# Self-attention in a two-block transformer kernel: one accumulator copy on ScalarE, and both halves of the first probability tile on GpSimd

## The chip, the core and the metric

The kernel runs on one core of a Trainium2 chip, in one launch. The metric is the time of one execution on the device, in microseconds (us). The engines are named as the profile names them: PE is TensorE (PEld its weight loads), DVE is VectorE, ACT is ScalarE, POOL is GpSimd, SP is SyncE, which here only issues DMAs. Each engine works through its own instructions in program order; between engines only semaphores set the order.

## What is computed

Eight sequences of 512 positions with 256 channels go through a cross-attention block (16 heads of 16 channels, context of 64 positions, with an MLP), then through a second block with self-attention, cross-attention and a gated MLP. The change lies in the self-attention of the second block, which is

```python
def _attn(xq, xc, Wq, Wk, Wv, Wo, bo):      # HEADS = 16, D_HEAD = 64
    q = (xq @ Wq).reshape(B, N, HEADS, D_HEAD)
    k = (xc @ Wk).reshape(B, S, HEADS, D_HEAD)
    v = (xc @ Wv).reshape(B, S, HEADS, D_HEAD)
    scores = jnp.einsum('bnhd,bshd->bhns', q, k) * scale
    attn = jax.nn.softmax(scores, axis=-1)
    out = jnp.einsum('bhns,bshd->bnhd', attn, v).reshape(B, N, HEADS * D_HEAD)
    return out @ Wo + bo

x = _attn(_ln(x, g1, b1), _ln(x, g1, b1), Wq1, Wk1, Wv1, Wo1, bo1) + x
```

with B = 8, N = S = 512.

## The kernel before, in words

**Numbers as pairs.** Every matrix product is made from float32 operands that are split in two: a rounded upper half (type fp32r) and the rest, the operand minus its rounded half. A product is three matmuls, upper x upper, upper x rest, rest x upper (`mm3`, lines 146 to 148). So every operand needs a rounded copy and a subtraction. The rounding of a tile is done by ScalarE (`act_copy`, line 156) or GpSimd (`pool_copy`, line 159), the subtraction by VectorE (`dve_rest`, line 162) or GpSimd (`pool_rest`, line 165).

**Steps.** The self-attention is a loop of steps (`loop3`), each for one sequence and one pair of heads: 8 x 8 = 64 steps. Step s works on three pairs at once: for u = s + 1 it projects queries, keys and values and takes the maxima of the scores; for t = s it makes scores less maxima and exponentials, in four tiles j = 0 to 3 of 128 keys by 2 x 512 queries; for d = s - 1 it multiplies the probabilities with the values. Normalization and output projection follow one to two steps later. The output projection is done for two pairs together, in two halves: the first in an odd step behind the value products of j = 3, the second in the next even step at j = 1. So steps of even and odd number differ. Every eighth step also makes a layer norm for a later sequence, and another one its statistics.

**TensorE**, in a step: score products for j (lines 1348 and 1352; the second adds the negated maxima), q projection, value products j = 0, k projection, values' projection, value products j = 1, in even steps a half of the output projection, four times the full scores for the maxima (line 1386; the first in bank 2 after j = 1), the value products of j = 2 and 3, in odd steps the other half of the output projection, and last four transposes of the maxima (line 152). The first product of line 1386 waits for the keys' rests (`k3_lo`); the output product of an odd step waits for the normalized halves (`o3_lo`).

**ScalarE**: rounded queries and keys (four copies of 64x512 after the exponential of j = 0), exponentials (line 1500), rounded values, the rounded probabilities of j = 1 and 2, and at j = 3 copies of the two accumulators: PSUM bank 4 holds the outputs of the first head in rows 0 to 63 and the sum of its probabilities in row 64, bank 5 the second head's outputs in rows 64 to 127 and its sum in row 0. Two copies of one row each go first and release the DMA of the sums (`d3_sum`), two copies of 64 rows gather both heads into one tile `OA` (`d3_out`). Behind them come the two copies of the negated maxima, which wait for the transposes, and the next step's queries.

**VectorE**: rests of the queries (line 1569), the reciprocals of the sums (1615), the subtraction for probability tile 3 of the step before, rests of the keys (1573) and of the values, the subtraction for tile 0 of this step, in even steps the residual addition (1636), maxima of two score tiles (1588), the subtraction for tile 1, two more maxima, in odd steps the residual addition, the subtraction for tile 2.

**GpSimd**: two copies of the rounded keys (64x512), the rounded probabilities of tile 0, then the normalization of an earlier pair: a multiplication by the reciprocals when these have landed (line 1697), a rounded copy and a rest; last the rounded probabilities of tile 3. The reciprocals are spread over 64 rows each by a DMA to memory and back (lines 1303 and 1307).

An exponential of tile j waits for the subtraction of tile j - 2, because there are two buffers `pst3` for the unrounded exponentials. The functions that the change touches, with what calls them:

## Time and profile before

| | us |
|---|---|
| median of 3 runs (2293.42 to 2293.97) | 2293.42 |
| the profiled execution's own time | 2292.69 |
| its span, first to last instruction | 2290.9 |
| TensorE busy | 2121.8 (93%) |
| VectorE busy | 1608.8 (70%) |
| ScalarE busy | 1482.3 (65%) |
| GpSimd busy | 1070.5 (47%) |

Busy times are those of the whole kernel, of which the self-attention is about half. "Idle before" in a row is the time for which an engine did nothing ahead of an instruction, with the engine, tile and line that ended it. A busy time of a VectorE or GpSimd row includes what the instruction waited inside itself.

### The profile page before, as it was taken

To read this page: it belongs to the slowest core of one execution; us is meant where nothing else is said; L and a number is where in the kernel's file an instruction comes from. 1 tells how busy PE (TensorE), PEld (TensorE's weight loads), DVE (VectorE), ACT (ScalarE), POOL (GpSimd) and SP (SyncE) were. 2 spreads that over 40 slices of the span, in tenths; PEclk is the share of its full clock that TensorE was granted. 3 is DMA by queue.
4 is the path that set the end of the run, shared out by engine and by line. 5 is a ranking of instruction groups with operands and counts; after the bars stand their busy time and mean duration, and the time that the engine had idled before them with its cause. 6 is when DMAs were issued, how large, how long until landed. Compare 5 with 4: busy or idle time off the path is not lost. (4 is left out here: it accounts for less than half of the span.)

```text
span 2290.9 us, 31305 instructions
## 1 busy us (share of the span) xinstructions
PE 2121.8 (93%) x11628; PEld 1771.6 (77%) x11628; DVE 1608.8 (70%) x2345; ACT 1482.3 (65%) x2154; POOL 1070.5 (47%) x819
## 2 busy tenths in 40 slices
PE   6868999988899999999999999999997799999998
PEld 4657888876687778777777777777776689888987
DVE  5576767753787787777877778778776766666553
ACT  5546888754777777777777777777774355554431
POOL 2154544441354454454544545545454665656432
PEclk8989999998999999999999999999999999999999
DMA  6810000010000100001001000010004411111000
GB/s 212 297 43 5 22 22 22 20 66 33 19 24 16 37 15 24 24 15 34 15 15 34 15 29 24 15 33 15 24 26 165 138 44 53 56 56 47 10 10 19
DMA packets 84280, 102.67 MB, mean 45 GB/s; under 512 B 29664, under 2 KB 61152, under 8 KB 83616
## 3 DMA queue, kind: packets, MB, share of 16 engines
q1 hardware_dynamic: 84128, 100.66, 13.3%
q8 instruction: 93, 1.52, 0.3%
q14 instruction: 59, 0.48, 0.1%
HBM read 65.50 MB, written 33.82 MB: 43 GB/s over the span
## 5 line engine op out<-in xcount | busy, mean ns | idle before, releaser
L146 PE MATMUL PS<-R 128*128 128x512 f32 (+1 forms) x2944 | 1026.4, 349 | 77.1 <-DVE R L162 46.1
L148 PE MATMUL PS<-R 128*128 128x512 f32 (+1 forms) x2944 | 996.5, 338 | 0.0
L147 PE MATMUL PS<-R 128*128 128x512 f32 (+1 forms) x2944 | 995.8, 338 | 0.0
L146 PEld LDWEIGHTS PS<-R 128*128 128x128 f32 x2944 | 565.8, 192 | 189.9 <-DVE R L162 55.3
L156 ACT ACTIVATE R<-PS 64x512 fp32r<-64x512 f32 (+4 forms) x860 | 460.1, 548 | 239.7 <-PE PS L1805 129.4
L148 PEld LDWEIGHTS PS<-R 128*128 128x128 f32 x2944 | 565.1, 192 | 60.4
L147 PEld LDWEIGHTS PS<-R 128*128 128x128 f32 x2944 | 566.9, 193 | 54.4
L162 DVE TENSOR_TENSOR R<-F,R 128x1024 fp32r<-128x1024 f32 (+2 forms) x416 | 465.2, 1123 | 44.2 <-ACT R L156 22.4
L159 POOL TENSOR_SCALAR R<-F 128x1024 fp32r<-128x1024 f32 (+1 forms) x295 | 266.2, 904 | 284.0 <-DVE F L1958 149.3
L1500 ACT ACTIVATE F<-PS 128x1024 f32<-128x1024 f32 x256 | 263.1, 1028 | 170.3 <-DVE R L162 115.1
L159 POOL TENSOR_SCALAR R<-R 64x512 fp32r<-64x512 f32 x128 | 142.8, 1129 | 391.4 <-ACT R L156 391.4
L1588 DVE TENSOR_REDUCE F<-PS 128x2 f32<-128x1024 f32 x256 | 301.4, 1214 | 14.1 <-PE PS L1386 14.1
L162 DVE TENSOR_TENSOR R<-PS,R 128x512 fp32r<-128x512 f32 (+3 forms) x348 | 181.0, 542 | 160.9 <-ACT R L156 160.3
L165 POOL TENSOR_TENSOR R<-F,R 128x512 fp32r<-128x512 f32 (+2 forms) x126 | 229.6, 1824 | 31.0 <-ACT R L156 22.4
L1569 DVE TENSOR_TENSOR R<-PS,R 64x512 fp32r<-64x512 f32 x128 | 88.0, 688 | 220.1 <-ACT R L156 220.1
L156 ACT ACTIVATE R<-F 128x1024 fp32r<-128x1024 f32 (+2 forms) x246 | 200.5, 829 | 61.2 <-PE PS L148 56.0
L156 ACT ACTIVATE F<-PS 64x512 f32<-64x512 f32 (+3 forms) x280 | 160.2, 593 | 50.4 <-PE PS L148 40.5
L1386 PE MATMUL PS<-R 128*128 128x512 f32 x512 | 164.0, 402 | 7.2 <-ACT F L156 4.9
L1352 PE MATMUL PS<-R 128*128 128x512 f32 x512 | 162.7, 399 | 7.8 <-ACT R L156 6.5
L1348 PE MATMUL PS<-R 128*128 128x512 f32 x512 | 165.9, 405 | 2.6 <-ACT F L1500 2.6
L1134 POOL TENSOR_TENSOR F<-F 128x1024 f32<-128x1024 f32 x32 | 67.9, 2123 | 165.4 <-DVE F L1048 165.4
L1697 POOL TENSOR_TENSOR F<-F 128x512 f32<-128x512 f32 x64 | 82.7, 1292 | 119.6 <-DMA F<-sd 119.6
(89 smaller groups left out, 1990.9 us busy)
## 6 DMA issues: line engine op xcount, KB each, us to landing
F<-sd SPq DMA_DIRECT2D x128, 128.0 KB, 2.8
xs<-F SPq DMA_DIRECT2D x16, 512.0 KB, 2.6
F<-xs SPq DMA_DIRECT2D x16, 512.0 KB, 3.6
gd<-F SPq DMA_DIRECT2D x8, 768.0 KB, 3.6
vd<-F SPq DMA_DIRECT2D x8, 768.0 KB, 5.9
R<-gd SPq DMA_DIRECT2D x6, 1024.0 KB, 5.5
R<-vd SPq DMA_DIRECT2D x6, 1024.0 KB, 5.7
F<-in_x SPq DMA_DIRECT2D x8, 512.0 KB, 5.7
```

The costliest lines, as they stand in the source:

```text
L146: nc.tensor.matmul(o, L[0], Rr[0], start=start, stop=False, skip_group_check=share)
L147: nc.tensor.matmul(o, L[0], Rr[1], start=False, stop=False, skip_group_check=share)
L148: return nc.tensor.matmul(o, L[1], Rr[0], start=False, stop=stop, skip_group_check=share)
L156: return nc.scalar.activation(o, i, ACT.Identity, **k)
L159: return nc.gpsimd.tensor_scalar(o, i, 1.0, 1.0, ALU.mult, ALU.mult)
L162: return nc.vector.tensor_tensor(o, i, f32(hi), ALU.subtract)
L165: return nc.gpsimd.tensor_tensor(o, i, f32(hi), ALU.subtract)
L1348: nc.tensor.matmul(bank(h), ka[i][h][:, kk], qa[i][h], start=True, stop=False)
L1352: m = nc.tensor.matmul(bank(h), kb[i][h][:, kk], qb[i][h], start=False, stop=True)
L1386: m = nc.tensor.matmul(bank(b0 + h), qa[i][h][:, 128 * q:128 * q + 128], ka[i][h], start=True, stop=True)
L1500: nc.scalar.activation(pst3[n % 2], bank(0, 2), ACT.Exp, scale=0.125).then_inc(e3.sem, 1)
L1588: nc.vector.tensor_reduce(M3[:, q, 0:128:64], bank(b0, 2).rearrange("p (a b) -> p a b", a=2), AX.X, ALU.max).then_inc(b3_max.sem, 1)
```

## The change

It does three things. ScalarE copies both accumulators whole in one instruction, `OAB <- bank(4, 2)`, 128x1024, instead of four; `OA` is then bank 4 and `OB` bank 5, and the DMAs take the sums from row 64 of `OA` and row 0 of `OB` once this copy is done. GpSimd multiplies the two heads apart, rows 0 to 63 of `OA`, and rows 64 to 127 from `OB` into `OA`. And GpSimd makes tile 0 of the probabilities whole, the rounded copy and now the subtraction too, both ahead of the keys' copies; VectorE's subtractions for tiles 1 to 3 stay. The event `p_lo` becomes two, one for each engine. TensorE's and SyncE's instructions keep their order.

```diff
--- before.py
+++ after.py
@@ -411,6 +411,7 @@
             o3_s = [ra.pair(NT) for _ in range(2)]
             wk = fa.take(6 * 512)
             pst3 = [wk[:, 1024 * i:1024 * i + 1024] for i in range(2)]
+            OAB = wk[:, 2048:3072]
             OA, OB = wk[:, 2048:2560], wk[:, 2560:3072]
             RS3 = fa.take(NT)
             M3 = fa.take(4, 128)
@@ -1197,8 +1198,9 @@
         nm3_mm, nm3_neg = event("nm_mm", N3), event("nm_neg", N3)
         c3_mm, e3 = event("c_mm", 4 * N3), event("exp", 4 * N3)
 
-        p3_act, p3_pool, p3_lo = event("p_act", 2 * N3), event("p_pool", 2 * N3), event("p_lo", 4 * N3)
-        d3_mm, d3_sum, d3_out = event("d_mm", 4 * N3), event("d_sum", N3), event("d_out", N3)
+        p3_act, p3_pool = event("p_act", 2 * N3), event("p_pool", 2 * N3)
+        p3_lo_pool, p3_lo_dve = event("p_lo_pool", N3), event("p_lo_dve", 3 * N3)
+        d3_mm, d3_out = event("d_mm", 4 * N3), event("d_out", N3)
         rec3, mul3, o3_hi, o3_lo = event("rec", N3), event("o_mul", N3), event("o_hi", N3), event("o_lo", N3)
         o3_mm, o3_add = event("o_mm", N3), event("x_add", N3)
         sum3 = [event(f"sum_in{i}", N3, 16) for i in range(2)]
@@ -1255,6 +1257,12 @@
             pool.wait_ge(vw_hi, 2 * b - 4 + half)
             v = vw_b[b % 2][:, 4 * half:4 * half + 4]
             pool_rest(v[:, :, 1], f32(v)[:, :, 1], v[:, :, 0]).then_inc(vw_lo.sem, 1)
+
+        def wait_rest3(queue, n):
+            if n % 4 == 0:
+                queue.wait_ge(p3_lo_pool, n // 4)
+            else:
+                queue.wait_ge(p3_lo_dve, 3 * (n // 4) + n % 4 - 1)
 
         def tail3(s, j):
 
@@ -1307,9 +1315,9 @@
                             nc.sync.dma_start(RS3[64 * h:64 * h + 64, :], sd[k][512 * h:512 * h + 512]
                                               .partition_broadcast(64)).then_inc(in3[k].sem, 16)
                     if ok(d, N3) and j == 3:
-                        sp.wait_ge(d3_sum, d)
+                        sp.wait_ge(d3_out, d)
                         sp.wait_ge(rec3, d - 2)
-                        nc.sync.dma_start(SQ3[d % 2][0:64, :], OB[64:65, :]).then_inc(sum3[d % 2].sem, 16)
+                        nc.sync.dma_start(SQ3[d % 2][0:64, :], OA[64:65, :]).then_inc(sum3[d % 2].sem, 16)
                         nc.sync.dma_start(SQ3[d % 2][64:128, :], OB[0:1, :]).then_inc(sum3[d % 2].sem, 16)
                     e = s - 3
                     if j == 1 and ok(e, N3) and e % 8 == 7:
@@ -1387,7 +1395,7 @@
                 m.then_inc(b3_mm.sem, 1)
 
             def values(d, j):
-                pe.wait_ge(p3_lo, 4 * d + j)
+                wait_rest3(pe, 4 * d + j)
                 pe.wait_ge(v3_lo, 2 * (d // 2) + j // 2)
                 if j == 0:
                     pe.wait_ge(d3_out, d - 1)
@@ -1496,7 +1504,7 @@
             def exponent(t, j):
                 n = 4 * t + j
                 act.wait_ge(c3_mm, n)
-                act.wait_ge(p3_lo, n - 2)
+                wait_rest3(act, n - 2)
                 nc.scalar.activation(pst3[n % 2], bank(0, 2), ACT.Exp, scale=0.125).then_inc(e3.sem, 1)
 
             def value(u):
@@ -1536,11 +1544,8 @@
                         act.wait_ge(d3_mm, 4 * d + 3)
                         act.wait_ge(sum3[(d - 1) % 2], 2 * ((d - 1) // 2) + 1)
                         wait_weights(act, "o1")
-                        act_copy(OB[64:65, :], bank(4)[64:65, :])
-                        act_copy(OB[0:1, :], bank(5)[0:1, :]).then_inc(d3_sum.sem, 1)
                         act.wait_ge(o3_lo, d - 1)
-                        act_copy(OA[0:64, :], bank(4)[0:64, :])
-                        act_copy(OA[64:128, :], bank(5)[64:128, :]).then_inc(d3_out.sem, 1)
+                        act_copy(OAB, bank(4, 2)).then_inc(d3_out.sem, 1)
                     if ok(u, N3) and j == 3:
                         act.wait_ge(nm3_mm, u)
                         act.wait_ge(c3_mm, 4 * (u - 2) + 3)
@@ -1574,12 +1579,12 @@
                                                 ).then_inc(k3_lo.sem, 1)
 
             def rests(n):
-                if 0 <= n < 4 * N3:
-                    if n % 4 in (1, 2):
+                if 0 <= n < 4 * N3 and n % 4 > 0:
+                    if n % 4 < 3:
                         dve.wait_ge(p3_act, 2 * (n // 4) + n % 4 - 1)
                     else:
-                        dve.wait_ge(p3_pool, 2 * (n // 4) + n % 4 // 3)
-                    dve_rest(P3[1][:, n % 4, :], pst3[n % 2], P3[0][:, n % 4, :]).then_inc(p3_lo.sem, 1)
+                        dve.wait_ge(p3_pool, 2 * (n // 4) + 1)
+                    dve_rest(P3[1][:, n % 4, :], pst3[n % 2], P3[0][:, n % 4, :]).then_inc(p3_lo_dve.sem, 1)
 
             def largest(u, q, b0):
                 dve.wait_ge(b3_mm, 4 * u + q)
@@ -1686,6 +1691,12 @@
                     for b_ in (6, 7):
                         pool.wait_ge(x_out[x_at(0, b_)], store_no[0, b_])
                 for j in range(4):
+                    if ok(t, N3) and j == 0:
+                        pool.wait_ge(e3, 4 * t)
+                        pool.wait_ge(d3_mm, 4 * (t - 1))
+                        pool_copy(P3[0][:, 0, :], pst3[0]).then_inc(p3_pool.sem, 1)
+                        pool.wait_ge(p3_pool, 2 * t)
+                        pool_rest(P3[1][:, 0, :], pst3[0], P3[0][:, 0, :]).then_inc(p3_lo_pool.sem, 1)
                     if ok(u, N3) and j == 0:
                         for h in range(2):
                             pool.wait_ge(k3_hi, 2 * u + h)
@@ -1694,16 +1705,23 @@
                         f = d - 1
                         pool.wait_ge(in3[f % 2], 2 * (f // 2) + 1)
                         pool.wait_ge(d3_out, f)
-                        nc.gpsimd.tensor_tensor(OA, OA, RS3, ALU.mult).then_inc(mul3.sem, 1)
+                        nc.gpsimd.tensor_tensor(OA[top, :], OA[top, :], RS3[top, :], ALU.mult)
+                        pool.wait_ge(o3_lo, f - 1)
+                        pool.wait_ge(p3_lo_pool, t) if more else pool.wait_ge(p3_pool, 2 * N3 - 1)
+                        if more and p == 5:
+                            pool.wait_ge(ln_rstd, 18 + b)
+                        if f == N3 - 1:
+                            pool.wait_ge(ln_nl, norm4[2][2])
+                        nc.gpsimd.tensor_tensor(OA[low, :], OB[low, :], RS3[low, :], ALU.mult).then_inc(mul3.sem, 1)
                         pool.wait_ge(mul3, f)
                         pool.wait_ge(o3_mm, 2 * ((f - 2) // 2) + 1)
                         pool_copy(o3_s[f % 2][0], OA).then_inc(o3_hi.sem, 1)
                         pool.wait_ge(o3_hi, f)
                         pool_rest(o3_s[f % 2][1], OA, o3_s[f % 2][0]).then_inc(o3_lo.sem, 1)
-                    if ok(t, N3) and j in (0, 3):
-                        pool.wait_ge(e3, 4 * t + j)
-                        pool.wait_ge(d3_mm, 4 * (t - 1) + j)
-                        pool_copy(P3[0][:, j, :], pst3[j % 2]).then_inc(p3_pool.sem, 1)
+                    if ok(t, N3) and j == 3:
+                        pool.wait_ge(e3, 4 * t + 3)
+                        pool.wait_ge(d3_mm, 4 * (t - 1) + 3)
+                        pool_copy(P3[0][:, 3, :], pst3[1]).then_inc(p3_pool.sem, 1)
                     for job in weights3_at(s, j):
                         pool_weight(job)
                     for _ in range(early4_pool.get(tail3(s, j), 0)):
@@ -1768,7 +1786,8 @@
             for i in loop4:
                 b = i // 4
                 if i == 2:
-                    sp.wait_ge(p3_lo, 4 * N3 - 1)
+                    wait_rest3(sp, 4 * N3 - 4)
+                    wait_rest3(sp, 4 * N3 - 1)
                     for k in range(4):
                         sp_weight(g5, k)
                     sp_load(3, 2, xs)
```

GpSimd in a step, before, from the keys' copies on (L159 R<-R) to the rounded copy of tile 3:

```order
L159 TENSOR_SCALAR R<-R 64x512 x2
L159 TENSOR_SCALAR R<-F 128x1024
L1697 TENSOR_TENSOR F<-F 128x512
L159 TENSOR_SCALAR R<-F 128x512
L165 TENSOR_TENSOR R<-F,R 128x512
L159 TENSOR_SCALAR R<-F 128x1024
```

GpSimd after; the first row holds the copy of tile 3 of one step and that of tile 0 of the next:

```order
L159 TENSOR_SCALAR R<-F 128x1024 x2
L165 TENSOR_TENSOR R<-F,R 128x1024
L159 TENSOR_SCALAR R<-R 64x512 x2
L1708 TENSOR_TENSOR F<-F 64x512
L1715 TENSOR_TENSOR F<-F 64x512
L159 TENSOR_SCALAR R<-F 128x512
L165 TENSOR_TENSOR R<-F,R 128x512
```

The copy of tile 0 moved from behind the keys' copies (L159 64x512 x2) to ahead of them, with a subtraction of 128x1024 (L165) behind it, and the multiplication (L1697) became two of 64x512 (L1708 and L1715).

VectorE in an even step before, from the rests of the queries (L1569) to the subtraction for tile 2:

```order
L1569 TENSOR_TENSOR R<-PS,R 64x512 x2
L1615 RECIPROCAL F<-F 128x8
L162 TENSOR_TENSOR R<-F,R 128x1024
L1573 TENSOR_TENSOR R<-PS,R 64x512 x2
L162 TENSOR_TENSOR R<-PS,R 128x4x64 x2
L162 TENSOR_TENSOR R<-F,R 128x1024
L1636 TENSOR_TENSOR F<-PS,F 128x512
L1588 TENSOR_REDUCE F<-PS 128x2 x2
L162 TENSOR_TENSOR R<-F,R 128x1024
L1588 TENSOR_REDUCE F<-PS 128x2 x2
L162 TENSOR_TENSOR R<-F,R 128x1024
```

VectorE in an even step after (its lines are numbered 5 higher, L1574 for L1569):

```order
L1574 TENSOR_TENSOR R<-PS,R 64x512 x2
L1620 RECIPROCAL F<-F 128x8
L162 TENSOR_TENSOR R<-F,R 128x1024
L1578 TENSOR_TENSOR R<-PS,R 64x512 x2
L162 TENSOR_TENSOR R<-PS,R 128x4x64 x2
L1641 TENSOR_TENSOR F<-PS,F 128x512
L1593 TENSOR_REDUCE F<-PS 128x2 x2
L162 TENSOR_TENSOR R<-F,R 128x1024
L1593 TENSOR_REDUCE F<-PS 128x2 x2
L162 TENSOR_TENSOR R<-F,R 128x1024
```

The L162 of 128x1024 between the values' rests (128x4x64) and the residual addition (L1641, before L1636) is gone; the one for tile 3 of the step before still stands behind the reciprocal and ahead of the keys' rests (L1578, before L1573).

## Rows read from the trace of the kernel before

**Rows 1.** Busy time in a stretch: us, each engine's busy us (x instructions), TensorE's clock, DMA.

```profile
573.40:1741.80 1168.40, 1119.05 (x5568) 901.96 (x5569) 905.03 (x1114) 880.11 (x1285) 564.65 (x472) 1.00 0.08 23
```

**Rows 2.** Waits, 800 to 1740 us: engine line waited for, us in total, times, longest us.

```profile
PEld PS L152 <- DVE F L1588: 29.0, 26, 1.7
...
PE PS L146 <- POOL R L165: 5.2, 9, 1.4
```

**Rows 3.** Timeline, VectorE, even step: start us, us, engine line op out<-in, [idle before].

```profile
1202.83 1.17 DVE L162 TENSOR_TENSOR R<-F,R 128x1024 fp32r<-128x1024 f32 x1
...
1206.38 1.21 DVE L162 TENSOR_TENSOR R<-F,R 128x1024 fp32r<-128x1024 f32 x1
1207.51 0.68 DVE L1636 TENSOR_TENSOR F<-PS,F 128x512 f32<-128x512 f32 x1
1208.11 2.35 DVE L1588 TENSOR_REDUCE F<-PS 128x2 f32<-128x1024 f32 x2
1210.37 1.82 DVE L162 TENSOR_TENSOR R<-F,R 128x1024 fp32r<-128x1024 f32 x1
```

**Rows 4.** Timeline, GpSimd, the same even step.

```profile
1202.78 2.29 POOL L159 TENSOR_SCALAR R<-R 64x512 fp32r<-64x512 f32 x2 [7.12 <-ACT R L156]
1205.03 1.05 POOL L159 TENSOR_SCALAR R<-F 128x1024 fp32r<-128x1024 f32 x1
1207.74 1.29 POOL L1697 TENSOR_TENSOR F<-F 128x512 f32<-128x512 f32 x1 [1.66 <-DMA F<-sd]
1209.12 0.62 POOL L159 TENSOR_SCALAR R<-F 128x512 fp32r<-128x512 f32 x1
1209.82 1.29 POOL L165 TENSOR_TENSOR R<-F,R 128x512 fp32r<-128x512 f32 x1
```

**Rows 5.** Timeline, ScalarE, the same even step.

```profile
1199.82 1.03 ACT L1500 ACTIVATE F<-PS 128x1024 f32<-128x1024 f32 x1
...
1213.63 2.27 ACT L156 ACTIVATE F<-PS 1x512 f32<-1x512 f32 x4
1215.92 2.41 ACT L156 ACTIVATE R<-PS 1x512 fp32r<-1x512 f32 x4
1218.36 1.03 ACT L1500 ACTIVATE F<-PS 128x1024 f32<-128x1024 f32 x1
```

**Rows 6.** Timeline, TensorE, the same even step.

```profile
1206.77 0.63 PE L1386 MATMUL PS<-R 128*128 128x512 f32 x2
...
1214.52 0.65 PE L152 MATMUL PS<-F 128*128 128x128 f32 x4 [0.93 <-DVE F L1588]
```

**Rows 7.** Timeline, VectorE, the odd step behind it.

```profile
1221.36 1.17 DVE L162 TENSOR_TENSOR R<-F,R 128x1024 fp32r<-128x1024 f32 x1
1222.56 1.41 DVE L1573 TENSOR_TENSOR R<-PS,R 64x512 fp32r<-64x512 f32 x2
...
1228.30 1.43 DVE L162 TENSOR_TENSOR R<-F,R 128x1024 fp32r<-128x1024 f32 x1
```

**Rows 8.** Timeline, GpSimd, the same odd step.

```profile
1226.67 1.29 POOL L1697 TENSOR_TENSOR F<-F 128x512 f32<-128x512 f32 x1 [2.05 <-DMA F<-sd]
...
1228.75 2.13 POOL L165 TENSOR_TENSOR R<-F,R 128x512 fp32r<-128x512 f32 x1
```

**Rows 9.** Timeline, TensorE, the same odd step.

```profile
1224.25 0.62 PE L1386 MATMUL PS<-R 128*128 128x512 f32 x2
...
1230.41 0.39 PE L148 MATMUL PS<-R 128*128 128x512 f32 x1
1231.03 0.36 PE L146 MATMUL PS<-R 128*128 128x256 f32 x1 [0.23 <-POOL R L165]
```

**Rows 10.** Timeline, all engines, a step with a layer norm.

```profile
1287.49 2.37 POOL L165 TENSOR_TENSOR R<-F,R 128x1024 fp32r<-128x1024 f32 x1
...
1288.16 2.79 DVE L162 TENSOR_TENSOR R<-F,R 128x1024 fp32r<-128x1024 f32 x1
```

**Rows 11.** Groups by form, GpSimd: line engine op shapes xcount, busy us, mean ns, idle before.

```profile
L165 POOL TENSOR_TENSOR R<-S,R 64x512 fp32r<-64x512 f32 x2 | 3.0, 1511 | 0.5 <-ACT R L156 0.5
```

## The prediction

> **What bounds the kernel now.** I read the profile in this order: where the self-attention lies, what TensorE waits for there, and then two neighbouring steps of it, row by row on each engine. Its 64 steps of four exponentials run from 573.4 to 1741.8 us: 1168.4 us, 18.3 us a step on average. In that stretch TensorE is busy for 1119 us at a granted clock of 1.00, VectorE for 905, ScalarE for 880 and GpSimd for 565 [rows 1]. So TensorE sets the pace, and only its waits can be won or added to. The waits of the steady part (940 us, 51 steps) name two places [rows 2]: the transposes (L152) wait for VectorE's last maximum (L1588), 29.0 us in 26 waits, 1.1 us in each step of even number; and a product of the output projection (L146) waits for GpSimd's L165, 5.2 us in 9 waits, all in odd steps. An earlier VectorE could win at the first place; the second shows how close GpSimd already is.
>
> **A rule of this kernel first: VectorE and GpSimd exclude each other.** In [rows 10] GpSimd's subtraction (L165, 128x1024) runs from 1287.49 to 1289.86. VectorE's subtraction (L162, both inputs in SBUF), which takes 1.17 to 1.21 us alone [rows 3], starts at 1288.16 and ends at 1290.95: 2.79 us, that is 1.09 us after GpSimd's end. The same in small: L162 at 1210.37 took 1.82 us behind L165 [rows 3, 4]. The other way round, L165 at 1228.75 met an L162 that ran from 1228.30 to 1229.73 and ended at 1230.88, 1.15 us after it, instead of after 1.29 us [rows 4, 7, 8]. Maxima and subtractions that read PSUM (L1588 at 1208.11, L1573 at 1222.56) are not stretched under a GpSimd instruction [rows 3, 4, 7]. The Trainium skill ("SBUF — State Buffer", section "Who interferes with whom") says the same: the pair is an exclusive lock, a VectorE instruction with two SBUF inputs contends with a GpSimd instruction that reads SBUF, and the later one is fully blocked; by that rule the trace agrees, and the rule speaks against this change.
>
> **Part 1: one copy by ScalarE.** Four copies of a row or half tile take 2.27 us [rows 5]; one of 128x1024 takes about what the exponential of that shape takes, 1.03 us. ScalarE saves 1.24 us a step. What it releases next are the two copies of the negated maxima, which wait for the transposes. In the even step the transposes end at 1214.52 + 0.65 = 1215.17 [rows 6], and the old copies at 1215.90. The row behind them holds the two maxima copies and two copies of the next q projection, from 1215.92 without a gap to the exponential at 1218.36 [rows 5]. With the short copy the maxima are through 0.7 us sooner, but TensorE ends that projection only at about 1217.0, just ahead of the 1217.12 at which ScalarE took it up: at most 0.1 us of the 1.24 is on the path. The sums leave for their DMA 0.14 us earlier, which nobody waits for: the reciprocal waits behind other VectorE work.
>
> **Part 2: both halves of tile 0 on GpSimd, ahead of the keys' copies.** VectorE loses one L162 of 1.21 us a step (1206.38, [rows 3]). GpSimd gets it as an L165 of 128x1024, 2.37 us [rows 10]. It now starts when the exponential ends: even step, exponential to 1200.85 [rows 5], 0.08 us on, copy of 1.05 us [rows 4] to 1201.98, 0.09 us on, subtraction from 1202.07 to 1204.44. VectorE's subtraction for tile 3 of the step before asks at 1202.83 [rows 3], inside that. It ends 1.09 us after 1204.44, at 1205.53 instead of 1204.00: **1.53 us late**. Behind it in VectorE's order stand the keys' rests (L1573), and TensorE's first score product for the maxima (L1386) waits for these. GpSimd was idle there before, until the keys' copies at 1202.78 [rows 4]; these now run to about 1207, and are not needed before the next step.
>
> **Part 3: the multiplication in two halves.** Half the partitions do not take half the time: 64x512 L165 took 1.51 us with its waits, 128x512 1.29 us [rows 4, 11]. So GpSimd's normalization becomes 1.29 us longer. Its start is set by the landing of the reciprocals (L1697 at 1207.74 and 1226.67), which should not move, for the reciprocal on VectorE (0.1 us ahead of L162) stands before the blocked subtraction and reads one small tile. Were it held as well, the landing would come 1.5 us later; that is counted with rival (c).
>
> **The even step, added up.** L1573 ends 1.53 us late, at 1206.97; TensorE wanted it for 1206.77 and starts at 1207.03 (+0.3). The residual addition (L1636) loses the L162 ahead of it and starts at 1206.38 + 1.53 = 1207.91 instead of 1207.51 [rows 3]. The two maxima behind it (1208.11, 2.35 us) then end at 1210.86, not 1210.46. The next L162 asks at 1210.77; GpSimd's second half multiplication ends at 1207.74 + 2 x 1.29 = 1210.32 and its copy of 0.62 us at 1211.02, so L162 ends at 1212.11 against 1212.19 before. The last maximum and with it the transposes move by -0.08 us. The 1.1 us wait stays: what was taken from VectorE is given back as blocked time. With the ScalarE part, -0.1 us a step.
>
> **The odd step, added up.** Here TensorE has no wait at the transposes, and no residual addition stands ahead of the maxima. Exponential to 1219.39 [rows 5], GpSimd's subtraction 1220.61 to 1222.98, VectorE's L162 ends at 1224.07 instead of 1222.53 [rows 7], L1573 1.54 us late at 1225.51. L1386 starts at 1225.57 instead of 1224.25 [rows 9]: +1.32. From there to the end of the value products TensorE needed 6.39 us (1224.25 to 1230.41 + 0.23), so these end at 1231.96; before, the output product started at 1231.03 because it waited for GpSimd: +0.9 from this side. GpSimd's side: multiplications from 1226.67 to 1229.25; VectorE's L162 asks at about 1228.8, goes first and ends at 1230.34; copy to 1230.84; subtraction from 1230.92 to 1232.21; output at 1232.36: +1.3. The later of the two holds, so **+1.3 us in this step**. The landing came 0.2 us later here, counted from the exponential (8.31 against 7.92 us), than in the even step; with the earlier landing it is +1.1. I take +1.2.
>
> **The sum.** Some 31 odd steps have an output: 31 x 1.2 = +37 us. 24 even steps x -0.1 = -2.4 us. In the 8 steps with a layer norm GpSimd is still in an addition of its own at the exponential's end, VectorE's L162 gets in first, and ScalarE's shorter copy counts for some 0.2 us: -1.6 us. The end of the stage has the longer multiplication and the shorter copy once each in its chain: 0, at most 2 either way. Together +33 us on the profiled execution's 2292.69 us (span 2290.9), or on the median of 2293.42 us: **2326 us**. Bounds of the parts: an odd step costs 0.9 (TensorE's side alone) to 1.5 us (both late landing and blocked copy), an even step -0.2 to +0.2 us: 2293.4 + 28 - 8 = 2313 to 2293.4 + 47 + 5 = 2345.
>
> **Rivals.** (a) *The long subtraction does not hold VectorE* there, or VectorE wins the port, as it did at 1202.83 against a GpSimd copy that had started at 1202.78 [rows 3, 4]. Then in even steps VectorE is really 1.2 us ahead, the residual addition starts when its product is there, at about 1207.1, the next L162 asks at 1210.1, waits for GpSimd's second half until 1210.32 and ends at 1211.41 instead of 1212.19, and the transposes come about 0.75 us earlier. In odd steps the halves of the multiplication still delay the output: VectorE's L162 then asks at 1227.5 and gets between the two halves (1227.96 to 1229.05), the second half ends at 1230.2, the subtraction at 1232.3: +1.3 again. Sum 31 x 1.3 - 32 x 0.75 = +16: 2310 us. Against it: GpSimd's subtraction starts 0.76 us before VectorE asks, not 0.05. (b) *Faster*: rival (a), and the halves do not reach the output either, because 64 partitions take half the time. Then even steps win 0.75 and odd ones nothing: 2293 - 24 = 2269 us. It decides at a half of 0.65 us; [rows 11] speaks against it. (c) *Slower still*: after the long subtraction GpSimd's next instruction, a keys' copy of 0.61 us, gets the port before VectorE does. Then 0.6 us more before L1573, which all 64 steps feel, or the reciprocal is held as said above, which the odd steps feel: some +25 to +35 us, 2350 to 2360. In [rows 10] VectorE was let in right after GpSimd's instruction, which speaks against it. (d) *Nothing moves*, since the waits swap exactly: it would need the odd steps' slack before L1386 to be 1.3 us; it was under 0.3 (L1573 ended at 1223.97, L1386 began at 1224.25).
>
> **Chances.** The forecast 0.61, (a) 0.16, (c) 0.11, (b) 0.08, nothing measurable 0.04. The range reaches from (a) with a little less, 2305, to the foot of (c), 2350; it leaves out (b), (d) and half of (c). A measurement of this kernel can tell about 0.2% (4.6 us) from no change. Faster, which is (b): 0.08; within 0.2%, (d): 0.04; slower, the forecast with (a) and (c): 0.88.
>
> **What would show it.** In the changed kernel's trace: VectorE's first 128x1024 subtraction of each step takes about 2.7 us instead of 1.17; TensorE's L1386 of odd steps waits some 1.3 us for L1573; the wait of the transposes stays near 1.1 us in even steps; odd steps take about 19.0 us and even ones about 18.4; ScalarE's busy time falls by 64 x 1.24 = 79 us with hardly any of it in the span. The prediction is wrong if that first subtraction keeps its 1.17 us, if a half multiplication takes 0.65 us, or if odd steps keep their length.

## The result, and the profile after

The changed kernel takes **2333.18 us** (median of 4 runs, 2331.58 to 2334.45) against 2293.42 us (4 runs, 2289.48 to 2293.97): 1.0177 times as long, 95% interval 1.0159 to 1.0194. It is 1.8% slower; 2326 had been forecast, in a range of 2305 to 2350.

The profiled execution has a span of 2330.9 us (2290.9 before) at the same mean granted clock of 0.98. Its page (busy time, its share of the span; then groups: line engine op out<-in, busy us, mean ns, idle before):

```profile
PE 2128.4 (91%) x11628; PEld 1784.3 (77%) x11628; DVE 1621.5 (70%) x2281; ACT 1398.8 (60%) x1962; POOL 1327.3 (57%) x947
...
L162 DVE TENSOR_TENSOR R<-F,R 128x1024 fp32r<-128x1024 f32 (+1 forms) x352 | 468.6, 1337 | 45.0 <-ACT R L156 25.2
L165 POOL TENSOR_TENSOR R<-F,R 128x1024 fp32r<-128x1024 f32 (+2 forms) x190 | 379.7, 2000 | 38.8 <-ACT R L156 24.9
L1508 ACT ACTIVATE F<-PS 128x1024 f32<-128x1024 f32 x256 | 262.8, 1027 | 197.3 <-DVE R L162 136.0
...
L1394 PE MATMUL PS<-R 128*128 128x512 f32 x512 | 165.8, 405 | 58.8 <-DVE R L1578 53.0
```

ScalarE's busy time fell from 1482.3 to 1398.8 us, 83.5 us for 64 steps, and TensorE's is the same within 7 us. The last row is what is new: TensorE now idles 58.8 us ahead of the full scores (L1394), where the same products (L1386) had 7.2 us before.

Where the 40 us lie is best read from step lengths: the distance from one step's first exponential row (L1500, L1508 after) to the next step's, averaged over a class of steps (first and last left out). "Stage" is the distance from the first step's to the last step's, "rest" what follows to the end of the span. "Even" leaves out the steps with a layer norm.

| us | even (x23) | odd (x31) | layer norm (x8) | stage | rest |
|---|---|---|---|---|---|
| before | 18.52 | 17.92 | 20.29 | 1161.3 | 556.1 |
| after | 18.46 | 19.21 | 19.76 | 1196.0 | 560.1 |

31 x 1.29 = 40.0, 8 x -0.53 = -4.2, 23 x -0.06 = -1.4 and the first step's 0.3 (17.56 to 17.89 us), which the averages leave out, make the stage's +34.7; the rest adds 4.0, and the stretch ahead of the stage 1.4 (573.4 to 574.8 us; it lies between 570.0 and 574.9 in all kernels of this study).

VectorE, after, an even step whose first exponential starts at 1219.07 (columns of this and the next rows: start us, us, engine line op out<-in, idle before). It answers [rows 3]:

```profile
1222.08 2.71 DVE L162 TENSOR_TENSOR R<-F,R 128x1024 fp32r<-128x1024 f32 x1
...
1227.16 0.68 DVE L1641 TENSOR_TENSOR F<-PS,F 128x512 f32<-128x512 f32 x1
1227.76 2.35 DVE L1593 TENSOR_REDUCE F<-PS 128x2 f32<-128x1024 f32 x2
1230.02 1.47 DVE L162 TENSOR_TENSOR R<-F,R 128x1024 fp32r<-128x1024 f32 x1
```

GpSimd in the same step, which answers [rows 4]:

```profile
1221.30 2.40 POOL L165 TENSOR_TENSOR R<-F,R 128x1024 fp32r<-128x1024 f32 x1
...
1227.07 1.28 POOL L1708 TENSOR_TENSOR F<-F 64x512 f32<-64x512 f32 x1 [1.23 <-DMA F<-sd]
1228.41 1.29 POOL L1715 TENSOR_TENSOR F<-F 64x512 f32<-64x512 f32 x1
1229.79 0.63 POOL L159 TENSOR_SCALAR R<-F 128x512 fp32r<-128x512 f32 x1
```

TensorE in the same step, which answers [rows 6]:

```profile
1226.37 0.70 PE L1394 MATMUL PS<-R 128*128 128x512 f32 x2 [0.19 <-DVE R L1578]
...
1233.81 0.66 PE L152 MATMUL PS<-F 128*128 128x128 f32 x4 [0.57 <-DVE F L1593]
```

GpSimd's subtraction runs from 1221.30 to 1223.70; VectorE's asks at 1222.08 and ends at 1224.79, 1.09 us after it: 2.71 us. The subtraction for tile 1 asks at 1230.02, 10.95 us after the exponential, and GpSimd's copy, which ends at 1230.42, holds it: it ends 1.07 us later. The transposes start 14.74 us after the exponential; before, 14.70 (1214.52 - 1199.82).

The odd step behind it starts at 1237.58. VectorE in it, which answers [rows 7]:

```profile
1240.59 2.73 DVE L162 TENSOR_TENSOR R<-F,R 128x1024 fp32r<-128x1024 f32 x1
1243.34 1.41 DVE L1578 TENSOR_TENSOR R<-PS,R 64x512 fp32r<-64x512 f32 x2
...
1248.15 1.22 DVE L162 TENSOR_TENSOR R<-F,R 128x1024 fp32r<-128x1024 f32 x1
```

GpSimd in the same odd step, which answers [rows 8]:

```profile
1239.83 2.40 POOL L165 TENSOR_TENSOR R<-F,R 128x1024 fp32r<-128x1024 f32 x1
...
1245.63 1.29 POOL L1708 TENSOR_TENSOR F<-F 64x512 f32<-64x512 f32 x1 [1.26 <-DMA F<-sd]
1246.98 1.29 POOL L1715 TENSOR_TENSOR F<-F 64x512 f32<-64x512 f32 x1
1248.35 1.49 POOL L159 TENSOR_SCALAR R<-F 128x512 fp32r<-128x512 f32 x1
1249.92 1.29 POOL L165 TENSOR_TENSOR R<-F,R 128x512 fp32r<-128x512 f32 x1
```

TensorE in the same odd step, which answers [rows 9]:

```profile
1244.90 0.70 PE L1394 MATMUL PS<-R 128*128 128x512 f32 x2 [1.62 <-DVE R L1578]
...
1251.11 0.39 PE L148 MATMUL PS<-R 128*128 128x512 f32 x1
1251.36 0.36 PE L146 MATMUL PS<-R 128*128 128x256 f32 x1
```

The full scores start 7.32 us after the exponential (5.89 before: 1224.25 - 1218.36) and have waited 1.62 us. The last value product starts at 1251.11, the output product of L146 at 1251.36 with no idle time ahead of it. GpSimd's subtraction ends at 1249.92 + 1.29 = 1251.21, 0.15 us before that product; the same 0.15 us lie between the two where TensorE visibly waits for GpSimd (before, 1230.88 and 1231.03). So both sides arrive at the same time here: in an odd step **two delays lie side by side**, and the later one counts. The output product starts 13.78 us after the exponential, against 12.67.

### The profile page after: what moved, and what is told of

The parts are those of the page before. It is cut to its first block and busy times, and to the rows that moved or that the text cites. A ratio compares the mean times of both kernels' runs of the same rounds, so it can differ in the third digit from the quotient of the medians.

```text
span 2330.9 us, 31241 instructions
## 1 busy us (share of the span) xinstructions
PE 2128.4 (91%) x11628; PEld 1784.3 (77%) x11628; DVE 1621.5 (70%) x2281; ACT 1398.8 (60%) x1962; POOL 1327.3 (57%) x947
## 5 line engine op out<-in xcount | busy, mean ns | idle before, releaser
L146 PE MATMUL PS<-R 128*128 128x512 f32 (+1 forms) x2944 | 1030.4, 350 | 73.6 <-DVE R L162 43.0
L146 PEld LDWEIGHTS PS<-R 128*128 128x128 f32 x2944 | 568.1, 193 | 182.8 <-DVE R L162 51.1
L148 PEld LDWEIGHTS PS<-R 128*128 128x128 f32 x2944 | 567.6, 193 | 61.2
L147 PEld LDWEIGHTS PS<-R 128*128 128x128 f32 x2944 | 569.5, 193 | 54.7
L159 POOL TENSOR_SCALAR R<-F 128x1024 fp32r<-128x1024 f32 (+1 forms) x295 | 303.8, 1031 | 468.8 <-ACT F L1508 246.6
L162 DVE TENSOR_TENSOR R<-F,R 128x1024 fp32r<-128x1024 f32 (+1 forms) x352 | 468.6, 1337 | 45.0 <-ACT R L156 25.2
L165 POOL TENSOR_TENSOR R<-F,R 128x1024 fp32r<-128x1024 f32 (+2 forms) x190 | 379.7, 2000 | 38.8 <-ACT R L156 24.9
L1508 ACT ACTIVATE F<-PS 128x1024 f32<-128x1024 f32 x256 | 262.8, 1027 | 197.3 <-DVE R L162 136.0
L162 DVE TENSOR_TENSOR R<-PS,R 128x512 fp32r<-128x512 f32 (+3 forms) x348 | 181.1, 543 | 160.2 <-ACT R L156 159.6
L1574 DVE TENSOR_TENSOR R<-PS,R 64x512 fp32r<-64x512 f32 x128 | 88.1, 688 | 209.4 <-ACT R L156 209.3
L1394 PE MATMUL PS<-R 128*128 128x512 f32 x512 | 165.8, 405 | 58.8 <-DVE R L1578 53.0
L1356 PE MATMUL PS<-R 128*128 128x512 f32 x512 | 166.2, 406 | 3.5 <-ACT F L1508 3.5
L1394 PEld LDWEIGHTS PS<-R 128*128 128x128 f32 x512 | 88.6, 188 | 101.1 <-issue 78.8
L159 POOL TENSOR_SCALAR R<-R 64x512 fp32r<-64x512 f32 x128 | 128.2, 1016 | 20.9 <-ACT R L156 20.9
L156 ACT ACTIVATE F<-PS 128x1024 f32<-128x1024 f32 (+2 forms) x88 | 81.7, 928 | 85.7 <-PE PS L148 57.3
```

The costliest lines, as they stand in the source:

```text
L146: nc.tensor.matmul(o, L[0], Rr[0], start=start, stop=False, skip_group_check=share)
L147: nc.tensor.matmul(o, L[0], Rr[1], start=False, stop=False, skip_group_check=share)
L148: return nc.tensor.matmul(o, L[1], Rr[0], start=False, stop=stop, skip_group_check=share)
L156: return nc.scalar.activation(o, i, ACT.Identity, **k)
L159: return nc.gpsimd.tensor_scalar(o, i, 1.0, 1.0, ALU.mult, ALU.mult)
L162: return nc.vector.tensor_tensor(o, i, f32(hi), ALU.subtract)
```

## Experiments

"A" and "B" in the expectations are the theory and its rival. Each table row is one kernel; the medians of the kernel before on the same chips were 2291.2 to 2291.6 us. The step lengths and the rest are those of the profiled execution, which took 4.7 us less than the median in e5 and 7.5 us less in e8, and in all others lay within 3.7 us of it.

| kernel | median us | ratio [95%] | even | odd | layer norm | rest |
|---|---|---|---|---|---|---|
| e1_one_copy | 2321.0 | 1.0129 [1.0114, 1.0144] | 17.93 | 19.11 | 19.88 | 562.4 |
| e2_tile0 | 2335.84 | 1.0195 [1.0178, 1.0212] | 18.87 | 19.15 | 20.11 | 556.9 |
| e3_behind_keys | 2324.17 | 1.015 [1.0133, 1.0167] | 17.84 | 19.38 | 19.77 | 562.2 |
| e4_tile0_behind | 2289.57 | 0.9992 [0.9982, 1.0001] | 18.36 | 18.02 | 20.04 | 556.1 |
| e5_one_mult | 2327.65 | 1.0153 [1.0134, 1.0171] | 18.52 | 19.13 | 19.60 | 554.9 |
| e6_keys_first | 2343.22 | 1.0219 [1.0196, 1.0241] | 18.51 | 19.22 | 21.10 | 563.4 |
| e7_memset | 2317.01 | 1.0107 [1.0091, 1.0122] | 17.89 | 19.11 | 19.77 | 561.5 |
| e8_both_removed | 2277.9 | 0.9931 [0.9909, 0.9952] | 17.72 | 18.00 | 19.59 | 558.4 |
| e9_version | 2265.16 | 0.9884 [0.9867, 0.99] | 17.42 | 17.98 | 19.63 | 554.1 |
| e10_no_gate | 2274.08 | 0.9922 [0.9894, 0.9951] | 17.92 | 18.00 | 19.61 | 553.8 |
| e11_gate_only | 2286.7 | 0.9975 [0.9965, 0.9984] | 18.24 | 18.03 | 20.06 | 557.1 |

**The two parts apart.** e1 is the kernel before with the one copy and the two multiplications, tile 0 as before; e2 is the kernel before with tile 0 whole on GpSimd ahead of the keys' copies, with four copies and one multiplication. The diffs of this section are cut to the instructions that count; waits are left out where "..." stands.

```diff
# e1: ScalarE, SyncE, GpSimd; the sum's DMA then reads OA[64:65]
-act_copy(OB[64:65, :], bank(4)[64:65, :])
-act_copy(OB[0:1, :], bank(5)[0:1, :]).then_inc(d3_sum.sem, 1)
-act_copy(OA[0:64, :], bank(4)[0:64, :])
-act_copy(OA[64:128, :], bank(5)[64:128, :]).then_inc(d3_out.sem, 1)
+act_copy(OAB, bank(4, 2)).then_inc(d3_out.sem, 1)
-nc.gpsimd.tensor_tensor(OA, OA, RS3, ALU.mult).then_inc(mul3.sem, 1)
+nc.gpsimd.tensor_tensor(OA[top, :], OA[top, :], RS3[top, :], ALU.mult)
 ...
+nc.gpsimd.tensor_tensor(OA[low, :], OB[low, :], RS3[low, :], ALU.mult).then_inc(mul3.sem, 1)
# e2: GpSimd, ahead of the keys' copies; VectorE's subtraction for tile 0 goes
+pool_copy(P3[0][:, 0, :], pst3[0]).then_inc(p3_pool.sem, 1)
 ...
+pool_rest(P3[1][:, 0, :], pst3[0], P3[0][:, 0, :]).then_inc(p3_lo_pool.sem, 1)
```

> Part 1 and 3 alone: the kernel before with ScalarE's one copy of both accumulators and GpSimd's multiplication in two halves; tile 0 as before. Theory A (the excluding of VectorE and GpSimd, and the longer chain of GpSimd, both count): in odd steps the output product waits for the longer chain, +1.2 us each in 31 steps; in even steps VectorE's subtraction for tile 1 asks while the second half runs and so gets in ahead of GpSimd's subtraction, which it did not before, and the transposes come 0.75 us earlier in 32 steps: 2293 + 37 - 24 = 2306 us. Theory B (the whole loss comes from tile 0's subtraction, the halves are hidden): no step longer, 2293 or less. Theory C (the halves alone cost the full 40 us): 2333.

> Part 2 alone: the kernel before with both halves of tile 0 on GpSimd ahead of the keys' copies; four accumulator copies and one multiplication as before. Theory A: VectorE's first 128x1024 subtraction takes 2.7 us in nearly all steps, odd steps +0.95 us from TensorE's L1386 (31 steps), even ones within 0.1: 2293 + 29 = 2322 us. Theory B (whole loss from here): 2333. Theory C (nothing from here): 2293.

e1 alone costs 1.3%, e2 alone 1.95%. In odd steps each costs nearly the whole (+1.19 and +1.23), and both together only 1.29: this is what two delays side by side look like. GpSimd in an odd step of e1 (first exponential at 1230.13):

```profile
1238.25 1.28 POOL L1695 TENSOR_TENSOR F<-F 64x512 f32<-64x512 f32 x1 [1.86 <-DMA F<-sd]
1239.59 1.29 POOL L1702 TENSOR_TENSOR F<-F 64x512 f32<-64x512 f32 x1
1240.97 1.48 POOL L159 TENSOR_SCALAR R<-F 128x512 fp32r<-128x512 f32 x1
1242.53 1.26 POOL L165 TENSOR_TENSOR R<-F,R 128x512 fp32r<-128x512 f32 x1
```

TensorE in the same step of e1:

```profile
1235.90 0.70 PE L1387 MATMUL PS<-R 128*128 128x512 f32 x2
...
1243.94 0.36 PE L146 MATMUL PS<-R 128*128 128x256 f32 x1 [1.40 <-POOL R L165]
```

The full scores start on time (5.77 us after the exponential), and it is GpSimd that TensorE waits for, 1.40 us ahead of the output product. In e2's odd steps the same product has no wait at all; there the full scores start 7.32 us after the exponential, behind an L162 of 2.72 us. VectorE and TensorE in such a step of e2 (first exponential at 1238.57):

```profile
1241.58 2.72 DVE L162 TENSOR_TENSOR R<-F,R 128x1024 fp32r<-128x1024 f32 x1
1245.89 0.70 PE L1393 MATMUL PS<-R 128*128 128x512 f32 x2 [1.29 <-DVE R L1580]
```

e2 costs more than the whole change because of its even steps: the same transposes, but ScalarE's four copies behind them. TensorE in an even step of e2 (first exponential at 1219.65):

```profile
1234.34 0.66 PE L152 MATMUL PS<-F 128*128 128x128 f32 x4 [0.53 <-DVE F L1595]
```

ScalarE in the same step of e2:

```profile
1233.85 2.27 ACT L156 ACTIVATE F<-PS 1x512 f32<-1x512 f32 x4 [0.43 <-PE PS L148]
1236.14 2.40 ACT L156 ACTIVATE R<-PS 1x512 fp32r<-1x512 f32 x4
1238.57 1.03 ACT L1507 ACTIVATE F<-PS 128x1024 f32<-128x1024 f32 x1
```

ScalarE is busy without a gap from 1233.85 to the next exponential. For e2, B was near (2333); for e1 I missed by 15 us (2306): the odd steps cost what they should, but the even ones won 0.59 us and not some 0.75 as in rival (a), and the rest grew by 6.3 us.

**The place of the subtraction.** In e3 (from after) and e4 (from e2) it moves behind the keys' copies.

```diff
 # GpSimd, j == 0
 pool_copy(P3[0][:, 0, :], pst3[0]).then_inc(p3_pool.sem, 1)
-pool_rest(P3[1][:, 0, :], pst3[0], P3[0][:, 0, :]).then_inc(p3_lo_pool.sem, 1)
 ...
 pool_copy(kb[u % 2][h][top, :], f32(ka[u % 2][h])[top, :]).then_inc(k3_dup.sem, 1)
+pool_rest(P3[1][:, 0, :], pst3[0], P3[0][:, 0, :]).then_inc(p3_lo_pool.sem, 1)
```

> The changed kernel with tile 0's subtraction on GpSimd moved behind the two keys' copies, where VectorE works from PSUM. Theory A: VectorE's first subtraction takes its 1.17 us again and L1386 has no wait; even steps 0.75 us shorter than before, odd ones still +1.3 us for the two halves: 2293 + 40 - 24 = 2309 us. Theory B (loss from GpSimd having the subtraction at all, wherever it stands): within 5 us of 2333. If the halves are hidden: 2270.

> The kernel before with tile 0's subtraction on GpSimd behind the two keys' copies, and four accumulator copies and one multiplication as before. Theory A: no block of VectorE there, the output chain as before. Odd steps unchanged; in even steps VectorE's subtraction for tile 1 asks within 0.1 us of GpSimd's subtraction for the output: 0.75 us shorter if VectorE gets in (2269 us), 0 if not (2293). Theory B (loss from GpSimd having the subtraction at all): about 2322 us, as with part 2 alone.

With the same instructions in another order, the 46 us of e2 are gone: e4 is at 0.9992. VectorE in an even step of e4 (first exponential at 1197.55):

```profile
1200.56 1.17 DVE L162 TENSOR_TENSOR R<-F,R 128x1024 fp32r<-128x1024 f32 x1
...
1207.71 2.25 DVE L162 TENSOR_TENSOR R<-F,R 128x1024 fp32r<-128x1024 f32 x1
```

GpSimd in the same step of e4:

```profile
1202.76 2.41 POOL L165 TENSOR_TENSOR R<-F,R 128x1024 fp32r<-128x1024 f32 x1
...
1207.59 1.29 POOL L165 TENSOR_TENSOR R<-F,R 128x512 fp32r<-128x512 f32 x1
```

The subtraction of 2.41 us lies where VectorE reads PSUM (keys' and values' rests, maxima), and L162 at 1200.56 has its 1.17 us. e3 came out at 2324 where 2309 was expected: the even steps gain 0.68, but GpSimd's chain to the output is longer still, since a half multiplication now meets VectorE's L162 (2.17 us at 1242.02, in the odd step from 1232.59), and the odd steps are 1.46 above before. TensorE's waits from 800 to 1740 us (columns as in [rows 2]) put it there:

```profile
PE PS L146 <- POOL R L165: 42.2, 31, 1.9
```

**The multiplication.** e5 is after with one multiplication of 128 rows, e8 the same with the subtraction behind the keys' copies.

```diff
-nc.gpsimd.tensor_tensor(OA[top, :], OA[top, :], RS3[top, :], ALU.mult)
 ...
-nc.gpsimd.tensor_tensor(OA[low, :], OB[low, :], RS3[low, :], ALU.mult).then_inc(mul3.sem, 1)
+nc.gpsimd.tensor_tensor(OA, OA, RS3, ALU.mult).then_inc(mul3.sem, 1)
```

> The changed kernel with one multiplication of all 128 rows of the first accumulator in place of the two halves (it leaves out the second head's own accumulator, so half of the attention output is not what it should be). It takes GpSimd's 1.29 us out of the output chain and leaves tile 0's subtraction ahead of the keys' copies. Theory A (in odd steps two delays lie side by side, each of about 1.3 us, and the later one holds): odd steps still 19.1 us, since TensorE's L1386 waits as before; the end of the stage 4 us shorter: 2327 to 2332 us. Theory B (the two delays add up): 31 x 0.65 less, about 2310. Theory C (the halves are the whole loss): 2293.

> The changed kernel with both suspected delays taken out: tile 0's subtraction behind the keys' copies, and one multiplication of all 128 rows (it leaves out the second head's own accumulator). ScalarE's one copy stays. Theory A: odd steps 17.9 us again, even ones 17.9 or less where VectorE gets in early, since with one copy ScalarE does not bind: 2293 - 20 = 2273 us, against 2290 for the same without the one copy. Theory B (a third cause is left): above 2293.

Taking away one of the two delays leaves the odd steps at 19.13 (e5) or 19.38 (e3); taking away both brings 18.00, and the time below the kernel before. e8 also shows what ScalarE's one copy is worth when nothing eats it: 2277.9 against e4's 2289.57. It is on the path with tile 0's subtraction ahead of the keys' copies too: e5 is e2 with the one copy, and its even steps are 0.35 us shorter (18.52 for 18.87), its layer-norm steps 0.51 (19.60 for 20.11). The rest of 554.9 us in e5, against 560.1, says that the longer end of the stage belongs to the halves: the kernels with two halves of the multiplication have a rest of 560.1 to 563.4 us, all others 553.8 to 558.4.

**What in the subtraction holds VectorE.** In e7 GpSimd writes the tile with three memsets instead, at the same place and for longer.

```diff
-pool_rest(P3[1][:, 0, :], pst3[0], P3[0][:, 0, :]).then_inc(p3_lo_pool.sem, 1)
+for _ in range(2):
+    nc.gpsimd.memset(f32(P3[1][:, 0, :]), 0.0).then_inc(pool_step.sem, 1)
+    pool.wait_ge(pool_step, pool_step.next())
+nc.gpsimd.memset(f32(P3[1][:, 0, :]), 0.0).then_inc(p3_lo_pool.sem, 1)
```

> The changed kernel with three memsets of the same tile, 3 x 0.95 = 2.85 us, in place of GpSimd's 2.4 us subtraction of tile 0 (it leaves out the rest of a quarter of the probabilities). GpSimd is busy for longer at the same place, but reads no SBUF. Theory A (VectorE's two-input subtraction is blocked by GpSimd's reading): VectorE's first subtraction of a step takes its 1.17 us again, L1386 has no wait, even steps 0.65 us shorter, odd ones held by the halves: 2293 + 40 - 20 = 2313 to 2324 us, like the variant with the subtraction behind the keys' copies. Theory B (any GpSimd work there, or its late keys' copies, delays the step): 2333 or more, first subtraction 2.7 us and above.

GpSimd in an even step of e7 (first exponential at 1209.48):

```profile
1211.70 1.97 POOL L1700 MEMSET R<- 128x1024 f32 x2
1213.72 0.96 POOL L1702 MEMSET R<- 128x1024 f32 x1
1214.64 1.20 POOL L159 TENSOR_SCALAR R<-R 64x512 fp32r<-64x512 f32 x2
```

VectorE in the same step of e7:

```profile
1212.49 1.17 DVE L162 TENSOR_TENSOR R<-F,R 128x1024 fp32r<-128x1024 f32 x1
```

L162 asks in the middle of 2.98 us of memsets and takes 1.17 us. So a busy GpSimd is not enough to hold VectorE; the instructions that held it in these traces, subtractions and copies, read SBUF, and the memset does not. The Trainium skill ("SBUF — State Buffer", section "Who interferes with whom") says just this: a VectorE instruction with two SBUF inputs contends with a GpSimd instruction that reads SBUF, and not with one that only writes it. The trace agrees: 1.17 us under the memsets, 2.71 us against the subtraction.

**Only the order on VectorE.** If the wait of the full scores were the whole cause, it would be enough to make the keys' rests ahead of the blocked subtraction. e6 is after with these two exchanged.

```diff
 # VectorE, j == 0
-rests(4 * s - 1)
 if ok(u, N3) and j == 0:
     project(u, 1)
+rests(4 * s - 1)
```

> The changed kernel with VectorE's keys' rests (two of 64x512, from PSUM) ahead of its blocked subtraction of tile 3. This takes the wait off L1386 of the maxima without touching GpSimd. Theory A: VectorE's subtraction still ends at 5.7 us after the exponential, so the exponential of j = 1 stays late and the scores of j = 2 start some 0.5 us late in odd steps; but GpSimd's halves hold the odd step at 19.1 us anyway; even steps 0.2 to 0.3 us shorter at most: 2325 to 2333 us. Theory B (L1386's wait is the whole cause): odd steps near 18, about 2297.

The full scores are back at 5.53 us after the exponential in odd steps, and nothing is won: 19.22. GpSimd's chain still holds the output, and the exponential of j = 1, which waits for L162, is no earlier (5.88 us, mean). TensorE's side has not become early either. It now waits at the scores of j = 2 (L1356), for that exponential; in the odd step of e6 from 1241.70:

```profile
1248.65 0.74 PE L1356 MATMUL PS<-R 128*128 128x512 f32 x2 [0.81 <-ACT F L1508]
```

In the odd steps the last value product starts 12.05 us after the first exponential before, 13.54 in after and 13.19 in e6 (means of 30 steps). So of the 1.49 us that VectorE's held subtraction costs TensorE there, 1.14 remain with the full scores on time: the delay takes two ways, over the keys' rests and over the exponential of j = 1.

The layer-norm steps got 1.3 us longer. VectorE in one of them (first exponential at 1298.83):

```profile
1303.39 1.98 DVE L162 TENSOR_TENSOR R<-F,R 128x1024 fp32r<-128x1024 f32 x1
```

GpSimd in it:

```profile
1301.88 2.40 POOL L165 TENSOR_TENSOR R<-F,R 128x1024 fp32r<-128x1024 f32 x1
```

ScalarE in it:

```profile
1305.46 1.03 ACT L1508 ACTIVATE F<-PS 128x1024 f32<-128x1024 f32 x1 [3.15 <-DVE R L162]
```

In after, L162 stood ahead of the rests, asked at 1297.95 in that step, just before GpSimd's subtraction of 1298.00, and was through in 1.17 us. One place later it meets the subtraction, and the exponential waits 3.15 us. So e6, at 2343, is slower than either theory had it.

**A version that is faster than both.** What e4 leaves is read from its even steps. The small subtraction of GpSimd (1207.59) holds VectorE's L162 for tile 1 (1207.71, 2.25 us, above), the transposes wait 1.21 us, and ScalarE's four copies are behind them. So e9 lets GpSimd wait in even steps until VectorE is through, and gives the two one-row copies of the sums to VectorE, which stands idle there. e10 has only the second edit, e11 only the first.

```diff
 # e9 and e11: GpSimd
 pool.wait_ge(o3_hi, f)
+if more and s % 2 == 0:
+    wait_rest3(pool, 4 * t + 1)
 pool_rest(o3_s[f % 2][1], OA, o3_s[f % 2][0]).then_inc(o3_lo.sem, 1)
 ...
 # e9 and e10: these leave ScalarE; VectorE, behind the last two maxima
+nc.vector.tensor_copy(OB[64:65, :], bank(4)[64:65, :])
+nc.vector.tensor_copy(OB[0:1, :], bank(5)[0:1, :]).then_inc(d3_sum.sem, 1)
```

> A version meant to keep what the change wins and leave its two delays: four accumulator copies and one multiplication as before, tile 0's subtraction on GpSimd behind the keys' copies; the two one-row copies of the sums by VectorE instead of ScalarE; and in even steps GpSimd's subtraction for the output waits for VectorE's subtraction of tile 1. Theory A: the transposes of even steps come 0.75 us earlier and ScalarE's chain behind them is 1.2 us shorter: even steps 17.85 us, odd ones as before: 2293 - 24 = 2269 us. If VectorE's two copies (0.7 us each) come into its own way: 2293 or more.

> The last version without GpSimd's added wait in even steps. Theory A: VectorE's subtraction of tile 1 then meets GpSimd's output chain (copy and subtraction, 9.4 to 11.4 us after the exponential) and is blocked as in the variant with tile 0 alone behind the keys' copies, where it took 2.10 us instead of 1.22: even steps 0.6 to 0.8 us longer than in the last version, 17.42 to about 18.1: 2265 + 20 = 2285 us. Theory B (the wait makes no difference, the sums by VectorE are the whole gain): 2265.

> The last version with the copies of the sums back on ScalarE, so GpSimd's added wait alone on top of tile 0's subtraction behind the keys' copies. Theory A: ScalarE binds even steps: from the end of the value products four copies, 2.27 us, then the negated maxima and the queries, so even steps 18.2 to 18.4 us although the transposes come 1.0 us earlier: 2283 to 2290 us. Theory B (ScalarE's copies are covered, as in the kernel before): 2265.

e9 takes **2265.16 us, 1.2% less than the kernel before** and 2.9% less than the changed one. VectorE in an even step of e9 (first exponential at 1185.99):

```profile
1189.01 1.17 DVE L162 TENSOR_TENSOR R<-F,R 128x1024 fp32r<-128x1024 f32 x1
...
1196.16 1.22 DVE L162 TENSOR_TENSOR R<-F,R 128x1024 fp32r<-128x1024 f32 x1
...
1199.67 0.69 DVE L1635 COPY F<-PS 1x512 f32<-1x512 f32 x1
```

TensorE in the same step of e9:

```profile
1199.70 0.66 PE L152 MATMUL PS<-F 128*128 128x128 f32 x4 [0.18 <-DVE F L1593]
```

ScalarE in the same step of e9:

```profile
1199.55 1.20 ACT L156 ACTIVATE F<-PS 64x512 f32<-64x512 f32 x2 [0.78 <-PE PS L148]
1200.78 1.19 ACT L156 ACTIVATE R<-PS 1x512 fp32r<-1x512 f32 x2
```

Neither L162 shown is held (in odd steps the one for tile 1 still is: 1.49 us, mean), the transposes start 13.71 us after the exponential (14.70 before), and the copies of the maxima are through at 1201.97. The parts are not additive: the wait alone (e11) gains 2.9 us on e4, because ScalarE's four copies bind there; with the sums moved it gains 8.9 us on e10. The even steps say the same: 0.12 us each for the wait alone (18.36 to 18.24), 0.50 with the sums moved (17.92 to 17.42). e10 was expected at 2285 and came at 2274: the moved copies are worth 15.5 us by themselves, more than I gave them.

## Why the prediction was right, and where it was off

- **The lock.** The first 128x1024 subtraction of each step was to take about 2.7 us and end 1.09 us after GpSimd's: 2.71 and 2.73 us in the steps shown, 2.64 and 2.72 us on average in even and odd steps. e7 shows that it is GpSimd's reading that does it; e4, that it goes when the place is changed.
- **The even step.** Forecast: L162 for tile 1 asks 10.95 us after the exponential (1210.77 - 1199.82), transposes 0.08 us earlier, together -0.1. Measured: 10.95; transposes 0.04 later in the steps shown; -0.06 a step. What left VectorE came back as blocked time. But this is right in part by luck: e2 and e5 show two terms that cancel. Tile 0 on GpSimd alone makes an even step 0.35 us longer (18.52 to 18.87 in e2), where the forecast had no loss: the full scores start 0.3 us late, as forecast, the value products end 0.40 us later (14.11 us after the exponential for 13.71, means), and ScalarE's four copies, which wait for them, are through 0.40 us later too. The one copy takes 0.35 us back (18.52 in e5), where at most 0.1 was given to it.
- **The odd step.** Both sides were named and the rule "the later holds" was right. GpSimd's side: half multiplications of 1.29 us each, the copy held by VectorE (1.49 us), as forecast; the reciprocals landed 0.26 us earlier than assumed, so +1.1 instead of +1.3 in the steps shown; e1 gives +1.19 for it alone. **TensorE's side was mis-sized**: 0.9 forecast, 1.11 in the steps shown and +1.23 in e2, where it stands alone. The full scores started 1.43 us late, not 1.32. The forecast had GpSimd 0.4 us behind TensorE; in the trace they arrive together. And the odd step that was picked had waited longer than most for GpSimd before, so that more of a delay was absorbed there: its output product started 12.67 us after the exponential, that of the median odd step 12.46 (13.79 in after). With 1.29 for 1.2, 31 steps give 40.0 instead of 37.
- **The layer-norm steps** won 0.53 us, not 0.2: -4.2 us for -1.6. The reason was right (VectorE's subtraction gets in first, 1.17 us). The shorter copy was sized too low: e4, with four copies, has 20.04 in these steps, and e8, with one, 19.59; e2 and e5 are 0.51 apart.
- **The end of the stage** was put at 0, at most 2; it is +4. TensorE in the last step with exponentials (the first at 1770.81), after:

```profile
1782.65 0.58 PE L146 MATMUL PS<-R 128*128 128x256 f32 x1 [2.82 <-POOL R L165]
```

Its output product starts 11.84 us after the exponential; before, 9.31 (1744.10 - 1734.79). GpSimd's two multiplications began 7.13 us after it (5.78 before, for the one) and took 1.2 us more. Here no maxima are left for TensorE, GpSimd's chain stands alone, and I had not read it. One rival is TensorE's granted clock: it stood at its lower level (1.2 GHz) for 30.7 us of the rest in after and for 22.2 us before, and in after one such stretch begins at 1781.8, during the wait shown. At half speed, the 8.5 us more would be worth up to about 4 us (an estimate). It is not all of it: e8, e2 and e11, with one multiplication, have 25.7, 27.9 and 28.1 us at the lower level and a rest of 558.4, 556.9 and 557.1 us; e3, with the halves, has 27.3 us and 562.2. So the halves cost some 4 to 5 us at about the same clock; how that divides over the last rounds and the stage behind them, and how much the clock adds in after, stays open.
- **ScalarE** lost 83.5 us of busy time (79 forecast). "Hardly any of it in the span" was wrong: from e2 to e5 the one copy shortens the stage by 12.3 us (1206.1 to 1193.8), nearly all in even and layer-norm steps. Against the kernel before that gain does not show, since tile 0's subtraction had lost 0.35 us in each even step.
- **The rivals.** (a), VectorE not held, is what e7 does: 2317 (2310 forecast). (b), faster, with halves of half the time, needs what e8 has: 2277.9 (2269 forecast). The halves took 1.28 and 1.29 us. (c) did not come: VectorE got its turn right after the subtraction, and the reciprocals landed 8.05 us after the exponential in the odd step (8.31 before).

The sum was 7 us short (33 us for 40.0 in the span): 3.0 from the odd steps, 1.0 from the even ones (-1.4 for -2.4), 4.0 from the end and 1.4 ahead of the stage, less 2.6 from the layer-norm steps.

## What to carry to other kernels

When work goes from VectorE to GpSimd, its place decides more than its length: lay each GpSimd instruction that reads SBUF where VectorE reads PSUM, not where VectorE has two SBUF inputs, and look for the pair in both directions. The same subtraction was worth -46 us here for being moved behind two copies. Where two engines both reach one product late, removing either delay alone shows little (-5.5 us in e5 and -9.0 in e3, and 0.08 us at most in an odd step); only the kernel without both (-55.3 us, e8), or each delay put alone into the kernel before, tells what they cost.

## What the runs showed of the hardware that I had not expected

- GpSimd's memsets of 2.98 us did not hold VectorE's two-input subtraction (1.17 us, e7), while a subtraction of 2.40 us at the same place stretched it to 2.71.
- Half the partitions save GpSimd nothing: 64x512 took 1.28 and 1.29 us, as 128x512 did (1.29), which was forecast. The same holds for its copies: two of 64x512 took 1.20 us (e7, 1214.64), one of 128x512 0.63 us (after, 1229.79).
- A ScalarE copy of 128x1024 from two PSUM banks took 1.02 us, where the two 64-row copies take 1.20 us together (e9, 1199.55).
